# Second attention of a two-layer decoder: the causal mask of the key-major scores as a select on POOL in place of a mask matmul

## The chip, the cores and the metric

One core of a Trainium2 chip. The metric is the device time of one execution in microseconds (us); the kernel before takes 373.02 us, the median of three runs (372.59 to 373.35).

## What is computed

A decoder of two layers on 8 sequences of 128 tokens with 128 features. Each layer is an attention, a cross attention on a context, and a feed-forward part, each followed by a residual add and a normalisation. The change lies in the first attention of the second layer ("the second attention"), 16 heads of 8 features, causal:

```
x = _layernorm(x + _L0_attn_ref(x, ...))      # 16 heads of 64
x = _layernorm(x + _L0_xattn_ref(x, ctx, ctx, ...))
x = _layernorm(x + _L0_ffn_ref(x, ...))       # gated by a softmax of 8
x = _layernorm(x + _L1_attn_ref(x, ...))
x = _layernorm(x + _L1_xattn_ref(x, ctx, ctx, ...))
x = _layernorm(x + _L1_ffn_ref(x, ...))       # quantised to whole numbers

# _L1_attn_ref
scores = jnp.einsum('bhqd,bhkd->bhqk', q, k) / jnp.sqrt(jnp.asarray(D, x.dtype))
causal = jnp.tril(jnp.ones((S, S), dtype=bool))
scores = jnp.where(causal, scores, -jnp.inf)
probs = jax.nn.softmax(scores, axis=-1)
out = jnp.einsum('bhqk,bhkd->bhqd', probs, v)
return out.transpose(0, 2, 1, 3).reshape(B, S, E) @ W_proj + b_proj
```

## The kernel before

Every engine has its program written out by hand, and all of them follow one table of ticks. The first attention takes ticks 0 to 31, one quad (four heads of one pair of sequences) a tick. The second attention begins at tick 32; below its ticks are counted from there as u. It takes the 8 sequences ("batches") one after the other, batch b from u = 4b on, and two ticks later from batch 4 on. A quad is again four heads of a batch, so 32 quads.

The batches come in groups. Groups 0, 1 and 2 hold batches 0 to 2, 3 to 5, and 6 and 7; for each of them a series of "mid" steps does the cross attention and the feed-forward part of layer 0, two normalisations among them, and the keys and queries of the second attention. These leave by DMA to HBM and come back as stacks, Kst and Qst, with high and low parts in rows. Late groups 3 and 4 (batches 0 to 3 and 4 to 7) do the rest of layer 1 in "late" steps. The function `plan` puts each step at a place of the tick table; an engine works through the same table in order and does its share of each step at that place.

A quad of the second attention passes through these steps:

- `scores1` with of_keys false (PE): a mask matmul of 512 columns (L668, ident_b times maskq), then per head one matmul (L676). VectorE takes the row maxima (L1234). After four quads TensorE turns the maxima (L707), and VectorE writes them negated to MR (L1093, L1094).
- `scores1` with of_keys true (PE), from five ticks after the query quad on: the same with keys as rows, so that the exponentials come out ready to be multiplied with the values. A mask matmul with maskk (L668), then per head the scores (L673) and the negated maximum (L674).
- the exponential on ScalarE (L963) into PT, a ring of three slots of 128x512 float32.
- `weigh1` (PE, L690), one tick after the scores of the quad: the exponentials times the values and a column of ones.
- every fourth quad ScalarE copies the sums out (L975), TensorE transposes them (L726), VectorE divides (L1246, L1249), and TensorE, ScalarE and VectorE project and add (L730, L970, L733, L1254).

TensorE's order within a tick is: steps of the table, scores of the query quad, turned maxima, scores of the key quad, steps of the table, `weigh1` and the output of a batch. The three banks 0 to 2 of PSUM go round over the query and key quads.

POOL (GpSimd) sets up constants, among them maskk (L385, L389), and then does only steps of the table: the inverse square root of the normalisations of groups 0 and 3 (`rsqrt`, 16 small instructions, L405 to L413), a sum of bias and rows (`add_bias`, L418), the clearing of the stacks (`zero`, L433), and the rounding of the last weights in three blocks (`ternary`, L425 to L427). For the other groups VectorE does the square root itself (L1155 to L1161). In the second attention's ticks POOL's table reads: `add_bias` of group 2 at u = 7, `zero(2)` at 8, `ternary(0)` at 9, `ternary(1)` at 16, `add_bias` at 21, `ternary(2)` at 22, `rsqrt` of group 3 at 25 and 31. Key quads are scored at u = 5 to 20 (batches 0 to 3) and 23 to 38 (batches 4 to 7).

ScalarE normalises group 3 for the second time at u = 34 (L910), behind its exponential of that tick. The late steps of group 4 begin with L744, which waits for all eight outputs of the second attention.

Of the kernel before, what the change touches and what calls it, by code (L numbers as in the profile page):

```python
# [5 lines left out]
ALU = mybir.AluOpType  # L6
# [8 lines left out]
P = 128  # L15
NB = 8
# [26 lines left out]
T1 = NQ  # L43
# [11 lines left out]
def decoder(nc, x_tok, x_T, ctx_T, wq0, wk0, wv0, wo0, xwq0, xbq0, xwk0, xbk0, xwv0, xbv0,  # L55
# [5 lines left out]
    with ExitStack() as ctx:  # L61
        def sb(name, shape, dt=F32):
            return ctx.enter_context(nc.sbuf_tensor(name, shape, dt))
# [24 lines left out]
        ident = sb("ident", [P, P])  # L88
        ident_b = sb("ident_b", [P, P], BF16)
        maskq = sb("maskq", [P, P], BF16)  # L90
        maskk = sb("maskk", [P, P], BF16)
        res = sb("res", [P, NB, P])
        stats = sb("stats", [P, NB, 6])
        mv = sb("mv", [P, NB, 2])
# [264 lines left out]
        def _(pool):  # L359
# [11 lines left out]
            for m in (ident, ident_b):  # L371
# [10 lines left out]
                               base=-32, pattern=[[-1, H], [0, P]], channel_multiplier=1)\  # L382
                .then_inc(s("setup"), 1)
            pool.memset(maskq[:], 0.0)
            pool.memset(maskk[:], 0.0)  # L385
            link(pool.memset(ones[:], 1.0))
            pool.affine_select(out=maskq[:], in_=maskq[:], compare_op=ALU.is_ge, fill=MASKED,
                               base=0, pattern=[[-1, P]], channel_multiplier=1)
            pool.affine_select(out=maskk[:], in_=maskk[:], compare_op=ALU.is_ge, fill=MASKED,  # L389
                               base=0, pattern=[[1, P]], channel_multiplier=-1)\  # L390
                .then_inc(s("masks"), 1)
            link(pool.memset(af[:, 12288:16384], 0.0))
            for v in VE:
# [73 lines left out]
            def run(t, k):  # L467

                for kind, g, i in TICKS.get((t, k), ()):
                    (mid if kind == "mid" else late)(g, i)  # L470

            for t in range(T1 + TICKS1):
                for k in range(3):
                    run(t, k)


        @block.tensor
        def _(pe):
# [177 lines left out]
            def scores1(w, b, q, of_keys):  # L656

                if w >= 3:
                    pe.wait_ge(s1_free[w % 3], w // 3)
                else:  # L660
                    pe.wait_ge(s("max_done"), NQ)
                g = GROUP[b]
                pe.wait_ge(s(f"stack_in{g}"), 128)
                if of_keys:
                    pe.wait_ge(s("mr1_done"), b + 1)
                t = slice((b - B0[g]) * P, (b - B0[g] + 1) * P)
                K, Q, dst = Kst[g], Qst[g], bank(w % 3)
                mm(dst, ident_b[:], (maskk if of_keys else maskq)[:].unsqueeze(1).broadcast_to([P, 4, P]),  # L668
                   start=True, stop=False)
                for h in range(4):  # L670
                    n, part_ = 4 * q + h, dst[:, h * P:(h + 1) * P]
                    if of_keys:
                        mm(part_, K[:, n, t], Q[:, n, t], start=False, stop=False)  # L673
                        m = mm(part_, En[:, n, :], MR[:, b % 2, :], start=False, stop=(h == 3))  # L674
                    else:
                        m = mm(part_, Q[:, n, t], K[:, n, t], start=False, stop=(h == 3))  # L676
                m.then_inc(s("scores1_done"), 1)

            def weigh1(b, q):

                v, w = 4 * b + q, k_use[b, q]
                pe.wait_ge(s1_free[w % 3], w // 3 + 1)
                if q == 0:
                    pe.wait_ge(s(f"ve_done{GROUP[b]}"), 1)
                    if b:
                        pe.wait_ge(s("o1_out"), b)
                for r in range(4):
                    g = GROUP[b]
                    n = (b - B0[g]) * H + 4 * q + r
                    m = mm(bank(3)[32 * r:32 * r + 32, q * P:(q + 1) * P], VE[g][:, 32 * n:32 * n + 32],  # L690
                           PT[:, v % SLOTS_PT, r * P:(r + 1) * P], start=True, stop=True)
                m.then_inc(s("pv1_done"), 1)
# [760 lines left out]
```

## Time and profile before

| | us |
|---|---|
| median of three runs | 373.02 |
| lowest, highest run | 372.59, 373.35 |
| span of the profiled execution | 371.0 |
| TensorE busy (PE) | 274.2, 74% |
| weight loads (PEld, beside PE) | 222.8, 60% |
| VectorE (DVE) | 250.2, 67% |
| ScalarE (ACT) | 170.9, 46% |
| GpSimd (POOL) | 62.9, 17% |

The profiled execution has a span of 371.0 us, from its first to its last instruction; the profile gives no other time of its own for it, and what lies around the span in the timed runs is 2.0 us (373.02 - 371.0). A busy share is the time in which an engine had an instruction in work. The durations of matmuls are modelled and overlap: the cost of one in a series is the distance from its start to the next start. PEld are weight loads, which run beside the matmuls. "idle before" in square brackets is the time that the engine had nothing to do, with what ended it. The granted clock (PEclk) is 1.00 at 2.4 GHz and 0.50 at 1.2 GHz.

### The profile page before, as it was taken

The numbers are of one execution on the slowest core, as the hardware profiler recorded it, in microseconds if no ns is written. First come the engines' busy times: TensorE is split into PE (matmuls) and PEld (weight loads), VectorE is DVE, ScalarE is ACT, GpSimd is POOL, SyncE is SP. The second block draws the span as 40 slices with busy tenths as digits, with TensorE's granted clock in tenths as the row PEclk, the third lists the DMA queues.
The fourth block names the chain that finished last, engine by engine and source line by source line (L and its number), as shares of the span: only waits on it lengthen the run. The fifth ranks groups of instructions, "written<-read, shape, count | busy, mean of one in ns | idle before, by whom it ended". The sixth has DMA issues, their size and how long they took to land.

```text
span 371.0 us, 6872 instructions
## 1 busy us (share of the span) xinstructions
PE 274.2 (74%) x2578; PEld 222.8 (60%) x2578; DVE 250.2 (67%) x694; ACT 170.9 (46%) x338; POOL 62.9 (17%) x137
## 2 busy tenths in 40 slices
PE   0957678988999989979866697987868874650440
PEld 0946668987899889979755364655545542330120
DVE  4974895589667987586777674657625566767574
ACT  5973663676357944714422343353323352412543
POOL 8700000000003103045150128003300300000300
PEclk9988999999999999989998699898989996975555
DMA  7941023000400050000420043000300000000001
GB/s 264 353 106 31 2 43 72 2 0 16 101 2 0 4 114 2 2 2 29 79 22 2 11 77 42 2 3 7 69 14 0 3 2 0 0 0 1 2 0 57
DMA packets 11568, 14.21 MB, mean 38 GB/s; under 512 B 1552, under 2 KB 9360, under 8 KB 11024
## 3 DMA queue, kind: packets, MB, share of 16 engines
q1 hardware_dynamic: 11536, 13.78, 15.7%
q8 instruction: 21, 0.34, 0.4%
q14 instruction: 11, 0.09, 0.1%
HBM read 8.01 MB, written 1.57 MB: 26 GB/s over the span
## 4 chain that ended last, share of the span: by engine, by line
PE 37%; DVE 34%; DMA 11%; ACT 10%; issue 6%; SPq 2%; ACTq 0%; DVEq 0%
DVE arena L1082 9%; PE PS L562 4%; DMA arena<-arena 4%; PE PS L522 4%; PE PS L588 3%; DMA q_piece<-VN 3%; DVE OT L1124 3%; ACT arena L877 3%; PE PS L485 2%; ACT xt L910 2%; DVE w0l L1071 2%; PE PS L668 2%; DMA arena<-q_piece 2%; DVE stats L1145 2%; PE PS L535 1%
## 5 line engine op out<-in xcount | busy, mean ns | idle before, releaser
L1082 DVE TENSOR_TENSOR arena<-PS,arena 64x512 f16<-64x512 f32 x64 | 44.0, 688 | 4.4 <-ACT arena L877 3.2
L504 PE MATMUL PS<-xh,w0l 128*128 128x256 f32 x96 | 31.5, 328 | 16.7 <-ACT w0h L861 9.3
L877 ACT ACTIVATE arena<-PS 64x512 f16<-64x512 f32 x64 | 37.9, 592 | 12.7 <-PE PS L506 12.0
L963 ACT ACTIVATE PT<-PS 128x512 f32<-128x512 f32 x32 | 19.1, 597 | 45.7 <-PE PS L674 45.7
L405 POOL TENSOR_SCALAR shift<-mv 128x3 f32<-128x3 f32 (+1 forms) x6 | 1.4, 232 | 206.9 <-DVE mv L1148 206.9
L562 PE MATMUL PS<-V,PT 128*128 128x96 f32 x256 | 33.9, 276 | 2.5 <-DVE On L1111 2.5
L562 PEld LDWEIGHTS PS<-V,PT 128*128 128x128 f32 x256 | 31.8, 194 | 3.0 <-ACT PT L897 2.8
L890 ACT ACTIVATE V<-PS 64x256 f32<-64x256 f32 x64 | 24.0, 375 | 19.3 <-PE PS L522 18.6
L504 PEld LDWEIGHTS PS<-xh,w0l 128*128 128x128 f32 x96 | 19.0, 198 | 19.8 <-ACT w0h L861 9.3
L1234 DVE TENSOR_REDUCE rowmax<-PS 128x4 f32<-128x512 f32 x32 | 21.8, 685 | 13.4 <-PE PS L676 13.3
L910 ACT ACTIVATE xt<-res,shift,rstd 128x128 f32<-128x128 f32 x42 | 17.7, 483 | 24.7 <-DVE shift L1161 24.7
L1124 DVE COPY OT<-PS 64x256 f32<-64x256 f32 x64 | 26.9, 420 | 1.4 <-PE PS L580 0.7
L1087 DVE TENSOR_REDUCE rowmax<-PS 128x4 f32<-128x512 f32 x32 | 22.0, 689 | 8.5 <-PE PS L536 8.0
L505 PE MATMUL PS<-xl,w0h 128*128 128x256 f32 x96 | 27.7, 289 | 0.0
L506 PE MATMUL PS<-xh,w0h 128*128 128x256 f32 x96 | 27.7, 288 | 0.0
L897 ACT ACTIVATE PT<-PS 128x512 f32<-128x512 f32 x32 | 19.1, 598 | 12.3 <-PE PS L551 11.3
L549 PE MATMUL PS<-arena 128*128 128x128 f16 x128 | 23.5, 222 | 0.1
L535 PE MATMUL PS<-arena 128*128 128x128 f16 x128 | 19.0, 228 | 6.0 <-DMA arena<-arena 4.8
L550 PE MATMUL PS<-arena 128*128 128x128 f16 x128 | 23.3, 220 | 0.0
L551 PE MATMUL PS<-MR,En 128*128 128x128 f16 x128 | 23.2, 220 | 0.0
L522 PE MATMUL PS<-ident,VN 128*64 128x128 f32 x128 | 21.2, 299 | 2.1 <-ACT VN L880 2.1
L505 PEld LDWEIGHTS PS<-xl,w0h 128*128 128x128 f32 x96 | 19.0, 198 | 0.1
(214 smaller groups left out, 702.6 us busy)
## 6 DMA issues: line engine op xcount, KB each, us to landing
arena<-arena SPq DMA_DIRECT2D x8, 512.0 KB, 4.1
arena<-k_piece SPq DMA_DIRECT2D x8, 96.0 KB
arena<-q_piece SPq DMA_DIRECT2D x8, 96.0 KB
xT<-x_T SPq DMA_DIRECT2D x1, 512.0 KB, 3.7
w<-wk SPq DMA_DIRECT2D x2, 256.0 KB, 4.5
w<-wq SPq DMA_DIRECT2D x2, 256.0 KB, 6.0
w<-wv SPq DMA_DIRECT2D x2, 256.0 KB, 6.3
wo<-wo SPq DMA_DIRECT2D x1, 512.0 KB, 7.0
```

The costliest lines, as they stand in the source:

```text
L504: mm(dst, w0l[:, w, g], xh[:, x], start=True, stop=False)
L505: mm(dst, w0h[:, w, g], xl[:, x], start=False, stop=False)
L506: m = mm(dst, w0h[:, w, g], xh[:, x], start=False, stop=True)
L522: m = turn(bank(at)[0:64, h * P:(h + 1) * P], VN[:, (4 * q + h) * 64:(4 * q + h + 1) * 64], ident[:])
L549: mm(dst, head(KA[p % 2], n), head(QB[p % 2], n), start=True, stop=False)
L550: mm(dst, head(KA[p % 2], n), head(QA[p % 2], n), start=False, stop=False)
L562: m = mm(bank(4)[:, h * VW:(h + 1) * VW], PT[:, Q % SLOTS_PT, h * P:(h + 1) * P], V[:, p % 2, 4 * q + h, :], start=True, stop=True)
L877: m = fn(dst[:, a], src[a * 64:(a + 1) * 64], ACT.Copy)
L890: m = fn(V[a * 64:(a + 1) * 64, p % 2, 4 * q:4 * q + 4, 0:DH0], src[:, :, a, :], ACT.Copy)
L910: fn(xt[:, b, :], res[:, b, :], ACT.Identity, bias=shift[:, b:b + 1], scale=rstd[:, b:b + 1]).then_inc(s(f"xn{g}"), 1)
L1082: m = tt(lower[:, a], src[a * 64:(a + 1) * 64], upper[:, a], ALU.subtract)
L1124: m = V_.tensor_copy(dst[a * 64:(a + 1) * 64, h, 4 * (o % 2):4 * (o % 2) + 4], src[h * 64:(h + 1) * 64, :, a])
```

## The change

The mask matmul of the key quads is gone. The scores of a key quad start each head's 128 columns afresh (start=True), so that ScalarE takes the exponential of unmasked scores. A new POOL instruction per quad then sets to zero every exponential whose key comes behind its query (an affine select on the 128x512 of the PT slot, in place), and `weigh1` waits for the select (semaphore p1_masked) where it waited for the exponential. The select of a tick stands behind the steps at the first place of the table and ahead of those at the second. The constant maskk is no longer made. The query quads keep their mask matmul.

```
-        maskk = sb("maskk", [P, P], BF16)
...
-            pool.memset(maskk[:], 0.0)
             link(pool.memset(ones[:], 1.0))
             pool.affine_select(out=maskq[:], in_=maskq[:], compare_op=ALU.is_ge, fill=MASKED,
-                               base=0, pattern=[[-1, P]], channel_multiplier=1)
-            pool.affine_select(out=maskk[:], in_=maskk[:], compare_op=ALU.is_ge, fill=MASKED,
-                               base=0, pattern=[[1, P]], channel_multiplier=-1)\
+                               base=0, pattern=[[-1, P]], channel_multiplier=1)\
                 .then_inc(s("masks"), 1)
...
+            def keep_causal(u):
+
+                for b in range(NB):
+                    if 5 <= u - u1(b) < 9:
+                        q = u - u1(b) - 5
+                        v, w = 4 * b + q, k_use[b, q]
+                        pool.wait_ge(s1_free[w % 3], w // 3 + 1)
+                        probs = PT[:, v % SLOTS_PT, :].rearrange("p (h q) -> p h q", h=4)
+                        pool.affine_select(out=probs, in_=probs, compare_op=ALU.is_ge, fill=0.0, base=0,
+                                           pattern=[[0, 4], [1, P]], channel_multiplier=-1)\
+                            .then_inc(s("p1_masked"), 1)
+
             for t in range(T1 + TICKS1):
-                for k in range(3):
-                    run(t, k)
+                run(t, 0)
+                if t >= TICKS0:
+                    keep_causal(t - T1)
+                run(t, 1)
+                run(t, 2)
+                if T1 <= t < TICKS0:
+                    keep_causal(t - T1)
...
-                mm(dst, ident_b[:], (maskk if of_keys else maskq)[:].unsqueeze(1).broadcast_to([P, 4, P]),
-                   start=True, stop=False)
+                if not of_keys:
+                    mm(dst, ident_b[:], maskq[:].unsqueeze(1).broadcast_to([P, 4, P]), start=True, stop=False)
...
-                        mm(part_, K[:, n, t], Q[:, n, t], start=False, stop=False)
-                        m = mm(part_, En[:, n, :], MR[:, b % 2, :], start=False, stop=(h == 3))
+                        mm(part_, K[:, n, t], Q[:, n, t], start=True, stop=False)
+                        m = mm(part_, En[:, n, :], MR[:, b % 2, :], start=False, stop=True)
...
-                v, w = 4 * b + q, k_use[b, q]
-                pe.wait_ge(s1_free[w % 3], w // 3 + 1)
+                v = 4 * b + q
+                pe.wait_ge(s("p1_masked"), v + 1)
```

The code behind it moves down by some lines, so the lines of POOL's helpers are four lower and those of the other engines 13 higher.

The order of POOL's instructions from u = 7 to u = 20, before. V MEMSET is `zero(2)`, and wgu_s and wo are the weights of `ternary`:

```order
L418 TENSOR_TENSOR w<-xt,bvx 128x256
L433 MEMSET V 128x4096
L425 TENSOR_SCALAR wgu_s<-wgu_s,wscl 128x512
L426 TENSOR_SCALAR wgu_s<-wgu_s 128x512
L427 TENSOR_SCALAR wo<-wgu_s 128x512
L425 TENSOR_SCALAR wgu_s<-wgu_s,wscl 128x512
L426 TENSOR_SCALAR wgu_s<-wgu_s 128x512
L427 TENSOR_SCALAR wo<-wgu_s 128x512
```

and with the change:

```order
L414 TENSOR_TENSOR w<-xt,bvx 128x256
L476 AFFINE_SELECT PT<-PT 128x512
L429 MEMSET V 128x4096
L476 AFFINE_SELECT PT<-PT 128x512
L421 TENSOR_SCALAR wgu_s<-wgu_s,wscl 128x512
L422 TENSOR_SCALAR wgu_s<-wgu_s 128x512
L423 TENSOR_SCALAR wo<-wgu_s 128x512
L476 AFFINE_SELECT PT<-PT 128x512 x7
L421 TENSOR_SCALAR wgu_s<-wgu_s,wscl 128x512
L422 TENSOR_SCALAR wgu_s<-wgu_s 128x512
L423 TENSOR_SCALAR wo<-wgu_s 128x512
L476 AFFINE_SELECT PT<-PT 128x512 x4
```

The selects are those of quad 3 of batch 0, quad 0 of batch 1, then seven up to quad 3 of batch 2, and the four of batch 3. The memset and the first two blocks of rounding, which followed each other, now stand between them.

The end of POOL's second `rsqrt` of group 3 (u = 31) and the beginning of its third (u = 57), before:

```order
L411 TENSOR_SCALAR nwt<-nwt 128x4
L412 TENSOR_TENSOR rstd<-nwt 128x4
L413 TENSOR_TENSOR shift<-shift,rstd 128x4
L405 TENSOR_SCALAR shift<-mv 128x4
L406 TENSOR_SCALAR nwt<-mv 128x4
```

and with the change:

```order
L407 TENSOR_SCALAR nwt<-nwt 128x4
L408 TENSOR_TENSOR rstd<-nwt 128x4
L409 TENSOR_TENSOR shift<-shift,rstd 128x4
L476 AFFINE_SELECT PT<-PT 128x512 x8
L401 TENSOR_SCALAR shift<-mv 128x4
L402 TENSOR_SCALAR nwt<-mv 128x4
```

The eight selects of batches 6 and 7 now stand behind the second `rsqrt`, the first of them being that of the same tick.

## Rows read from the trace of the kernel before

**Rows 1.** The chain that ended last, in order of time: start us, us, what

```profile
224.37 6.84 DMA arena<-q_piece
...
248.53 0.27 DVE rec L1246
...
267.95 3.67 DMA V<-q_piece
...
296.43 0.97 ACT xt L910 x3
...
313.50 2.08 PE PS L744 x2
```

**Rows 2.** Timeline, PE and ACT, one plain tick: start us, us, engine, instruction, count

```profile
275.92 0.22 PE L674 MATMUL PS<-MR,En 128*128 128x128 f16 x1
...
276.17 0.60 ACT L963 ACTIVATE PT<-PS 128x512 f32<-128x512 f32 x1 [1.79 <-PE PS L674]
...
276.88 0.38 PE L668 MATMUL PS<-maskk,ident_b 128*128 128x512 bf16 x1
...
277.09 0.22 PE L673 MATMUL PS<-arena 128*128 128x128 f16 x1
...
277.63 0.43 PE L690 MATMUL PS<-PT,arena 128*32 128x128 f32 x8
```

**Rows 3.** Busy time by stretch: PE, PEld, DVE, ACT, POOL, then PEclk, DMA share, GB/s

```profile
272.20:275.40 3.20, 3.20 (x26) 1.91 (x25) 0.75 (x2) 0.60 (x1) 0.00 (x0) 0.50 0.02 5
```

**Rows 4.** Timeline, POOL, the selects of the setup

```profile
1.31 0.29 POOL L372 TENSOR_SCALAR_AFFINE_SELECT ident<-ident 128x128 f32<-128x128 f32 x1 [0.25 <-POOL ident_b L370]
...
5.98 2.66 POOL L379 TENSOR_SCALAR_AFFINE_SELECT En<-En 128x2048 f16<-128x2048 f16 x1
...
11.62 0.72 POOL L387 TENSOR_SCALAR_AFFINE_SELECT maskq<-maskq 128x128 bf16<-128x128 bf16 x1
```

**Rows 5.** Timeline, DVE and POOL, where both work at once, and a step of DVE's square root

```profile
6.68 2.49 DVE L1071 TENSOR_TENSOR w0l<-w,w0h 128x512 fp32r<-128x512 f32 x1
...
239.67 0.16 DVE L1159 TENSOR_TENSOR nwt<-nwt 128x2 f32<-128x2 f32 x1
...
265.92 0.69 DVE L1298 TENSOR_TENSOR arena<-w 128x512 f32<-128x512 f32 x1
265.92 0.75 POOL L411 TENSOR_SCALAR nwt<-nwt 128x4 f32<-128x4 f32 x1
```

**Rows 6.** Timeline, POOL, during the second attention

```profile
221.24 3.52 POOL L433 MEMSET V<- 128x4096 f32 x1
224.74 0.70 POOL L425 TENSOR_SCALAR wgu_s<-wgu_s,wscl 128x512 f32<-128x512 f32 x1
...
227.71 0.70 POOL L425 TENSOR_SCALAR wgu_s<-wgu_s,wscl 128x512 f32<-128x512 f32 x1
...
290.38 0.23 POOL L405 TENSOR_SCALAR shift<-mv 128x4 f32<-128x4 f32 x1 [20.91 <-DVE mv L1148]
...
294.60 0.20 POOL L413 TENSOR_TENSOR shift<-shift,rstd 128x4 f32<-128x4 f32 x1
```

**Rows 7.** Timeline, ACT's exponentials and PE, where both meet the work of rows 6

```profile
221.66 0.60 ACT L963 ACTIVATE PT<-PS 128x512 f32<-128x512 f32 x1 [1.16 <-PE PS L674]
...
243.85 0.60 ACT L963 ACTIVATE PT<-PS 128x512 f32<-128x512 f32 x1 [1.20 <-PE PS L674]
...
289.38 0.60 ACT L963 ACTIVATE PT<-PS 128x512 f32<-128x512 f32 x1 [4.56 <-PE PS L674]
...
227.94 0.43 PE L690 MATMUL PS<-PT,arena 128*32 128x128 f32 x8
...
231.34 0.58 PE L668 MATMUL PS<-maskq,ident_b 128*128 128x512 bf16 x1 [1.71 <-DMA arena<-q_piece]
...
247.48 0.42 PE L690 MATMUL PS<-PT,arena 128*32 128x128 f32 x8
...
291.69 0.43 PE L690 MATMUL PS<-PT,arena 128*32 128x128 f32 x8
```

## Prediction

> **What bounds the kernel now.** I read the table of busy shares first, then the chain of waits in order of time, then the timelines of single engines where the second attention runs. The chain shows three stretches in the 90 us that the change touches. Twice TensorE stands still until the stacks of keys and queries of a group have arrived by DMA [rows 1]: for group 1 at 231.21, for group 2 at 271.62. Between and behind these it passes through ticks of TensorE, small VectorE steps (248.53), and at 296.43 ScalarE's second normalisation of late group 3. At 313.50 begins the work that waits for the whole second attention. What the change gives or takes must therefore show before 313.50, and what it takes before 267.95 delays the transfer of group 2 as well, since that transfer starts from the normalised rows of group 2.
>
> In a plain tick TensorE never waits for the exponentials. The last score matmul of a quad starts at 275.92, its exponential runs from 276.17 for 0.60, and the weighing matmul L690 of that quad starts at 277.63, behind the next tick's scores [rows 2]. So there is room of 277.63 - 276.77 = 0.86 us between exponential and use, and the select has to go into it.
>
> **What is taken away.** The mask matmul of the keys issues at 276.88 and the next matmul at 277.09 [rows 2]: 0.21 us of TensorE, 32 times, 6.7 us in all. (The 0.38 of the row is pipelined length.) In stretches where the granted clock is 0.50, as in 272.20 to 275.40 [rows 3], I count twice that, 0.42. Also gone are a 128x128 memset and a 128x128 select in the first 13 us, which nothing waits for until tick 1: nothing. Masks count only where TensorE is on the path. In front of the two DMA waits, and where a normalisation or a row maximum is awaited, they only lengthen a wait. I count as on the path: quad 3 of batch 1 (0.42), quad 0 of batch 2 (0.21), quad 3 of batch 2 (0.21), then quad 3 of batch 4 and quad 0 of batch 5 (0.42 each, at half clock), quad 1 of batch 5 (0.21), and quads 2 and 3 of batch 6 (0.21 each). That is 2.3 us. Quads 0 and 1 of batch 3 would count too (0.4), but they lie behind the wait worked out below, and are lost there.
>
> **What one select costs.** No row has a select of 128x512 float32. The nearest are 0.29 us for 128 elements a partition and 2.66 us for 2048 [rows 4]. A straight line between them gives 0.76 at 512; the 2.66 began while VectorE was busy on two SBUF operands, so I take 0.7. The far end is the 0.72 us of the old mask's own select, the same comparison on only 128 elements [rows 4]: four times that is 2.9 us. I don't take it, because it ran while VectorE's L1071 was going, and the next paragraph shows what that does. The low end is 0.29 + 0.3 = 0.6. A handover costs about 0.08: from 290.38 to 294.60 POOL makes 15 chained steps, 0.28 from start to start, of which 0.20 is the step [rows 6]. From the last score matmul to the weighing: 0.25 + 0.60 + 0.08 + 0.70 + 0.08 = 1.71 us. Before, the weighing came 1.71 after it (277.63 - 275.92), now 1.50 without the mask: in a plain tick 0.2 us of wait eats the 0.21 us won. Most ticks hold another step in the middle and have the room. The select alone is thus about neutral.
>
> The Trainium skill (GPSIMD Engine Reference, "Performance pitfalls for Q7 kernels") gives 2.03 cycles an element for a compare-and-select body that isn't unrolled; as an estimate from it a select would take 0.9 us, and each of the three queue waits below would be 0.2 longer. No run here shows it, and the 2048-element row stands against it.
>
> **What VectorE and POOL do to each other.** L1071 at 6.68 took 2.49 us, where the same shape takes 0.69 in L1298; it ended at 9.17, 0.53 behind the POOL select of 5.98 to 8.64. The other way round, POOL's L411, a step of the same size, took 0.75 at 265.92, exactly while that L1298 (two operands in SBUF) ran [rows 5]. So the two exclude each other for whole instructions. VectorE's reciprocal square root is a row of eleven such small steps, one of them at 239.67 [rows 5], and every later step of its group waits for it. A select that falls into it costs up to 0.7. One falls into the row around 239.67, one or two into the next one, ahead of group 2's transfer. I take 0.5 for the first and 0.4 for the second. The Trainium skill (SBUF — State Buffer, "SBUF: two separate sides") calls the shared port pair an exclusive lock held for the full instruction; by it each of these would be 0.7, and the sum 0.5 us higher. The trace agrees that there is such a lock.
>
> **What is queued on POOL.** This carries the forecast. POOL works in order, and in the order of the change long work stands ahead of selects for which TensorE waits.
>
> First, the memset of 3.5 us and the first 2.97 us block of weight rounding (start to start 224.74 to 227.71) [rows 6]. They ran from 221.24 on. Now the memset comes behind the select of quad 3 of batch 0, whose exponential ends at 222.26 [rows 7], so at 223.0. Then memset 3.5, select 0.8, rounding 3.0, select 0.8: 231.1 is the earliest for the weighing that started at 227.94. TensorE then did 1.69 us of steps, some of it waiting for ScalarE, and stood idle for 1.71 until the DMA's quad at 231.34 [rows 7]. With 1.1 us for those steps, ScalarE being free by then, that quad starts at about 232.2: **+0.9** (it would be +1.5 with the full 1.69).
>
> Second, the second rounding block now comes behind the select of quad 3 of batch 2 (exponential from 243.85) and ahead of that of quad 0 of batch 3. 243.85 + 0.60 + 0.08 + 0.70 + 2.97 + 0.08 + 0.70 + 0.08 = 249.1 against 247.48 [rows 7]: **+1.6**, and the transposes behind it feed VectorE's 248.53 and, over the normalisation, group 2's transfer.
>
> The third rounding block stands ahead of a select too, but in ticks in which no key quad is in flight, and the first square root of group 3 runs inside TensorE's wait for the DMA that ends at 271.62: nothing for either.
>
> Third, the second square root of group 3. It starts when VectorE has its moments (290.38) and ends at 294.80 [rows 6]. The select of quad 0 of batch 6 stands behind it, though its exponential was done at 289.98 [rows 7]. 294.80 + 0.08 + 0.70 + 0.08 = 295.7, against 291.69 for the weighing before [rows 7]: **+4.0**. Behind that weighing TensorE has two more ticks of scores, and ScalarE takes the normalisation at 296.43 only behind the exponential of quad 3 of batch 6; so it moves by all of it. The select lies behind moments that themselves don't wait for it, so nothing circles.
>
> TensorE's clock: behind the 4 us standstill that ends at 271.62 the granted clock was 0.50 for 3.2 us [rows 3]. A new standstill of 4 us should bring the same: two ticks with some 1.5 us of path work become longer. I take **+0.6**, between 0 and 1.5.
>
> **The sum**, in us: +0.9 +1.6 +4.0 (queue), +0.5 +0.4 (VectorE held up), +0.6 (clock), -2.3 (masks) = +5.7. Against the profiled span of 371.0 that is 376.7. The median of the runs is 373.0, 2.0 above the span; so the runs should come to 378.7. Unknowns: the select (0.6 to 0.8) moves it by 0.3 either way, the clock -0.6 to +0.9, the holding up -0.9 to +0.7, and delays that cover each other could take 2.
>
> **Rivals.** (a) *Faster*: POOL's work is early enough, TensorE never waits, the masks are pure gain. Then 2.3 + 0.4 = 2.7 us go: 370.3. For it: POOL is idle most of the stage. Against it: it needs the square root to leave POOL before 290.9, and it can't start before 290.38 [rows 6]. The deciding point is that select; chance 0.07, for an order or a wait that I misread. (b) *The late stall is covered*: if the normalisation at 296.43 were released by something that doesn't pass through the blocked weighing, +4.0 and +0.6 fall away: 1.1 over, 374.1. Chance 0.08. (c) *The comparison itself is slow*: 2.9 us a select, 32 of them are 93 us of POOL, about all the time from shortly before the first row of [rows 7] to 313.50; POOL becomes the bound, ticks of about 2 us become 3, some 20 us more, 395. The rows on the lock explain its 0.72 otherwise: chance 0.03. (d) Gains and waits cancel within 0.2%: 0.04.
>
> **How the numbers follow.** The forecast, both stalls with their sizes, has 0.78. A measurement of this kernel can tell about 0.2%, 0.75 us, from no change. Faster by more is (a), 0.07; within is (d), 0.04; slower is the forecast, (b) and (c), 0.89. The range takes in (b), so it begins at 373.8, and at the other end the bounds of the forecast, 382.5. It leaves out (a), (c) and most of (d), 0.14 together, and the far tails of the forecast.
>
> **What would show it.** Right: selects L476 with a mean near 0.7; TensorE idle ahead of L690 (its new line L703), released by POOL, longest about 4 us near 295; a POOL square root of group 3 directly ahead of it; a smaller one near 247; the normalisation of group 3 at about 302 instead of 296.43; the tail from the end of the second attention as long as before. Wrong: no wait of over 1 us behind POOL, or selects of 1.5 us and more, or the stage before 271 getting shorter.

## The result and the profile after

The change is slower: 382.97 us, the median of four runs (380.34 to 385.22), against 373.19 us for the kernel before, also the median of four. The ratio is 1.0248, 95% interval 1.0188 to 1.0308, so 9.3 us (7.0 to 11.5). Here and in the experiments the medians are over all executions of a kernel, and the ratios leave out the few that took over 1.5% longer than its fastest. The forecast was +5.7 and 378.7: the direction and the mechanism came as forecast, the size was too small. The median lies 0.5 above the range's upper end of 382.5; the ratio, applied to the 373.02 us of the forecast, gives 382.3, just inside.

The four executions were 380.34, 381.22, 384.72 and 385.22 us, with mean granted clocks of 0.879, 0.880, 0.866 and 0.866: the two long ones are those with the lower clock.

The page of the changed kernel's profiled execution (the slowest of the four, 385.22; span 383.4):

```profile
span 383.4 us, 6838 instructions
...
PE 276.4 (72%) x2546; PEld 224.8 (59%) x2546; DVE 253.4 (66%) x694; ACT 171.4 (45%) x338; POOL 82.1 (21%) x167
...
PEclk9986999999999999999978998698889596687555
...
L476 POOL TENSOR_SCALAR_AFFINE_SELECT PT<-PT 128x512 f32<-128x512 f32 x32 | 20.7, 650 | 50.1 <-ACT PT L976 50.1
```

TensorE has 32 mask matmuls fewer and yet 2.2 us more busy time (276.4 against 274.2): part of its work ran at half clock. The PEclk row of the kernel before reads

```profile
PEclk9988999999999999989998699898989996975555
```

A slice is about 9.3 us there and 9.6 in the changed kernel. Before, the row falls to 6 at 204 to 213 us, where normalised rows are awaited, and next at 306 to 315. Now it shows 6 at 240 to 249, 5 at 297 to 307, and 6 twice from 316 to 335. The mean granted clock is 0.866; the median of the runs of before in the experiments is 0.89.

Who waits for the select, first from the view of its own line, then among TensorE's waits from 200 to 345 us (total us, times, longest us):

```profile
L476 POOL TENSOR_SCALAR_AFFINE_SELECT PT<-PT x32: 634/634/852, 216.3 to 314.6; 128x512 f32<-128x512 f32 x32
...
who waited for it (us, times):
  PEld PS L703: 9.2, 6
  PE PS L703: 8.1, 5
```

```profile
PE PS L703 <- POOL PT L476: 8.1, 5, 3.9
```

Of 32 selects, 27 cost TensorE no wait. Five make 8.1 us, but only three of these, 7.0 us together, stand behind other work of POOL: those of quads 0 and 1 of batch 1 and of quad 0 of batch 6. The other two, 0.22 and 0.81 us, are waits for selects that began as soon as their exponential was done (quads 0 and 3 of batch 7). POOL's timeline shows what stands ahead of the three; it answers to [rows 6]:

```profile
223.03 0.63 POOL L476 TENSOR_SCALAR_AFFINE_SELECT PT<-PT 128x512 f32<-128x512 f32 x1 [0.81 <-ACT PT L976]
223.61 3.51 POOL L429 MEMSET V<- 128x4096 f32 x1
227.07 0.63 POOL L476 TENSOR_SCALAR_AFFINE_SELECT PT<-PT 128x512 f32<-128x512 f32 x1
227.69 0.70 POOL L421 TENSOR_SCALAR wgu_s<-wgu_s,wscl 128x512 f32<-128x512 f32 x1
...
229.17 1.50 POOL L423 TENSOR_SCALAR wo<-wgu_s 128x512 bf16<-128x512 f32 x1
230.63 1.22 POOL L476 TENSOR_SCALAR_AFFINE_SELECT PT<-PT 128x512 f32<-128x512 f32 x2
...
294.30 0.23 POOL L401 TENSOR_SCALAR shift<-mv 128x4 f32<-128x4 f32 x1 [4.86 <-DVE mv L1161]
...
298.49 0.20 POOL L409 TENSOR_TENSOR shift<-shift,rstd 128x4 f32<-128x4 f32 x1
298.63 1.23 POOL L476 TENSOR_SCALAR_AFFINE_SELECT PT<-PT 128x512 f32<-128x512 f32 x2
```

And TensorE's timeline, the rows with a wait at the same places and at the steps of the chain behind them ([rows 1, 7] before):

```profile
227.76 0.43 PE L703 MATMUL PS<-PT,arena 128*32 128x128 f32 x8 [1.52 <-POOL PT L476]
231.32 0.43 PE L703 MATMUL PS<-PT,arena 128*32 128x128 f32 x8 [1.66 <-POOL PT L476]
...
243.62 0.45 PE L743 MATMUL PS<-ident,V 128*128 128x128 f32 x1 [2.42 <-DVE V L1262]
...
275.41 0.58 PE L682 MATMUL PS<-maskq,ident_b 128*128 128x512 bf16 x1 [4.06 <-DMA V<-q_piece]
...
299.32 0.65 PE L703 MATMUL PS<-PT,arena 128*32 128x128 f32 x8 [3.86 <-POOL PT L476]
...
309.03 0.43 PE L703 MATMUL PS<-PT,arena 128*32 128x128 f32 x8 [0.22 <-POOL PT L476]
...
315.28 0.42 PE L703 MATMUL PS<-PT,arena 128*32 128x128 f32 x8 [0.81 <-POOL PT L476]
...
324.11 2.07 PE L757 MATMUL PS<-cT,wx 128*128 128x512 f32 x2 [0.45 <-DVE res L1267]
...
334.61 2.04 PE L766 MATMUL PS<-xT,wx 128*128 128x512 f32 x2 [0.78 <-ACT xT L928]
```

The first standstill behind POOL begins 1.5 us before the weighing at 227.76; the second releases at 231.32, where the forecast had worked out 231.1. The largest is at 299.32: the last instruction of the square root begins at 298.49, the select at 298.63, and 0.7 us later TensorE goes on. Of the 12.4 us that this profiled execution is longer than the one before, 3.65 are there when group 2's transfer arrives (275.41 against 271.76), 10.6 when L744, now L757, starts (324.11 against 313.50 in [rows 1]), and the rest comes in the tail. (1.1 us are there before the first select; another profile of the same kernel, below, hasn't got them.) The 0.81 at 315.28 costs nothing further on: from the last exponential to ScalarE's copy of the sums (L975, L988) it takes 3.43 us before and 3.44 now.

Step by step, the same weighing (L690, L703) comes later than before by 0.58 us at 240.78, 3.43 at 249.35, 3.58 at 251.06, 3.70 at 292.98, 7.63 at 299.32 (behind the late wait) and 10.31 at 307.57 (the end of batch 6). So the late wait adds 3.9, and the 8 us behind it add another 2.7, in which no new wait for POOL falls.

Between these places the clock changed. Busy time by stretch (us, then PE, PEld, DVE, ACT, POOL, granted clock, DMA share, GB/s), of the kernel before and then of the changed one:

```profile
243.00:250.00 7.00, 7.00 (x92) 4.97 (x92) 3.76 (x13) 3.13 (x7) 0.00 (x0) 1.00 0.01 4
...
296.40:303.00 6.60, 5.46 (x71) 3.68 (x71) 3.62 (x14) 4.73 (x12) 0.00 (x0) 1.00 0.01 2
```

```profile
243.60:250.60 7.00, 6.45 (x49) 4.54 (x50) 2.18 (x8) 2.56 (x6) 3.92 (x5) 0.53 0.01 2
275.40:281.20 5.80, 5.79 (x51) 3.81 (x52) 1.38 (x2) 1.79 (x3) 1.27 (x2) 0.52 0.00 0
...
294.00:299.30 5.30, 0.62 (x8) 0.45 (x8) 1.38 (x6) 0.77 (x2) 3.79 (x18) 0.88 0.00 0
299.30:309.00 9.70, 8.96 (x77) 5.96 (x77) 3.28 (x8) 4.31 (x10) 2.46 (x4) 0.54 0.01 2
```

Before, the stage from 290 to 303 ran at 1.00. Now TensorE does 0.62 us of work in 5.30 us, and behind that the clock stays near half for 9.7 us of nearly full work. The same 7 us behind L730 (L743) that held 92 matmuls now hold 49 (the counts of the two rows). The kernel before has more stretches at half clock than the 3.2 us of [rows 3], and a longer one among them, behind a wait of 4.68 us that ends at 207.69 (the clock is 0.50 from 207.6 on, 5.9 us in all):

```profile
208.60:213.50 4.90, 4.86 (x14) 2.69 (x15) 2.05 (x5) 1.66 (x3) 0.88 (x1) 0.50 0.06 20
```

The standstill ahead of L743 is behind VectorE, not POOL. In VectorE's square root, about 241 us, there is one step that took 0.60 where its equals take 0.16 ([rows 5]: 239.67), beside the POOL select that runs from 241.55 for 0.63. Its first step took 0.30 for 0.17, beside the select of 239.73 to 240.36:

```profile
240.08 0.30 DVE L1168 TENSOR_SCALAR nwt<-mv 128x2 f32<-128x2 f32 x1
...
241.41 0.16 DVE L1172 TENSOR_TENSOR nwt<-nwt 128x2 f32<-128x2 f32 x1
241.60 0.60 DVE L1173 SCALAR_TENSOR_TENSOR nwt<-nwt 128x2 f32<-128x2 f32 x1
242.23 0.16 DVE L1171 SCALAR_TENSOR_TENSOR nwt<-nwt 128x2 f32<-128x2 f32 x1
```

The reciprocal L1259 and the division L1262 stand behind it on VectorE, and TensorE waits for L1262 until 243.62: its standstill there grew from 1.41 to 2.42 us, and the half-clock stretch is what follows. Of the 1.01 us, 0.57 are the two steps held up (0.44 and 0.13). The other 0.43 are TensorE itself: measured from the start of the square root (239.07 before, 240.08 now) it comes to its wait 0.43 earlier, as much as two mask matmuls of 0.21. So three causes were to be told apart: POOL's queue, VectorE held up by POOL, and the clock.

### The profile page after: what moved, and what is told of

It reads as the page before. It is cut to its first block, busy times and chain, and to the rows that moved or that the text cites. A ratio compares the mean times of both kernels' runs of the same rounds, so it can differ in the third digit from the quotient of the medians.

```text
span 383.4 us, 6838 instructions
## 1 busy us (share of the span) xinstructions
PE 276.4 (72%) x2546; PEld 224.8 (59%) x2546; DVE 253.4 (66%) x694; ACT 171.4 (45%) x338; POOL 82.1 (21%) x167
## 4 chain that ended last, share of the span: by engine, by line
PE 38%; DVE 32%; ACT 11%; DMA 8%; issue 7%; POOL 2%; SPq 1%; ACTq 0%; DVEq 0%
DVE arena L1095 7%; ACT arena L890 4%; PE PS L535 4%; DMA arena<-arena 3%; PE PS L575 3%; PE PS L601 3%; DVE OT L1137 3%; PE PS L498 2%; ACT xt L923 2%; DVE stats L1158 2%; PE PS L517 2%; PE PS L703 2%; DMA w<-wq 1%; DVE arena L1280 1%; PE PS L548 1%
## 5 line engine op out<-in xcount | busy, mean ns | idle before, releaser
L476 POOL TENSOR_SCALAR_AFFINE_SELECT PT<-PT 128x512 f32<-128x512 f32 x32 | 20.7, 650 | 50.1 <-ACT PT L976 50.1
L910 ACT ACTIVATE PT<-PS 128x512 f32<-128x512 f32 x32 | 19.1, 597 | 10.7 <-PE PS L564 9.6
```

## The experiments

The changed kernel once more and eleven variants ran in three sets, the rows of the table in groups of four, each set with its own runs of the kernel before. "Clock" is the median over the runs of the mean granted clock. A difference of two ratios of this table is uncertain by about 0.0045, 1.7 us (2.2 with early_three, whose own interval is wider).

| | median us | before | ratio, 95% interval | clock |
|---|---|---|---|---|
| again | 384.14 | 373.1 | 1.0314 (1.0280 to 1.0349) | 0.866 |
| late_two | 377.81 | 373.1 | 1.0138 (1.0101 to 1.0174) | 0.881 |
| early_three | 381.3 | 373.1 | 1.0260 (1.0210 to 1.0309) | 0.873 |
| both_five | 376.64 | 373.1 | 1.0066 (1.0026 to 1.0106) | 0.887 |
| no_key_mask | 373.62 | 373.66 | 0.9975 (0.9940 to 1.0009) | 0.881 |
| idle_selects | 378.6 | 373.66 | 1.0130 (1.0091 to 1.0168) | 0.891 |
| before_filled | 371.0 | 373.66 | 0.9940 (0.9909 to 0.9971) | 0.903 |
| both_five_filled | 371.0 | 373.66 | 0.9913 (0.9883 to 0.9943) | 0.904 |
| change_filled | 378.36 | 374.13 | 1.0121 (1.0089 to 1.0152) | 0.905 |
| idle_selects_filled | 373.06 | 374.13 | 0.9976 (0.9948 to 1.0004) | 0.908 |
| no_key_mask_filled | 369.35 | 374.13 | 0.9892 (0.9861 to 0.9923) | 0.901 |
| before_filled_more | 367.79 | 374.13 | 0.9821 (0.9784 to 0.9858) | 0.934 |

### The change again: again

No edit.

> The changed kernel as it is, for its spread. Every theory: 9 to 10 us over before (382 to 383); single runs 380 to 385. If the spread comes from TensorE's clock, its runs with a low mean granted clock are the long ones.

384.14 us, 1 us more than expected, 1.0314: the change costs 11.7 us here (10.4 to 13.0), which overlaps the 9.3 of the first measurement (7.0 to 11.5). Four of its six executions have a clock of 0.866 or less, like the two long ones there, and the shortest of the six (382.8) has the highest, 0.875. It is the yardstick of the next three, which ran beside it.

### Back to the mask matmul where POOL is late: late_two, early_three, both_five

The quads in BY_MATMUL keep their mask matmul, wait for the exponential, and have no select. The three kernels differ in that list alone:

```
+BY_MATMUL = ((6, 0), (6, 1))                                   (late_two)
+BY_MATMUL = ((1, 0), (1, 1), (3, 0))                           (early_three)
+BY_MATMUL = ((1, 0), (1, 1), (3, 0), (6, 0), (6, 1))           (both_five)
...
+                        if (b, q) in BY_MATMUL:
+                            continue
                         pool.wait_ge(s1_free[w % 3], w // 3 + 1)
...
-                if not of_keys:
+                by_mm = not of_keys or (b, q) in BY_MATMUL
+                if by_mm:
```

> The changed kernel, but quads 0 and 1 of batch 6, whose selects stand behind POOL's second square root of group 3, keep the mask matmul and have no select. Theory queue: the wait of 3.9 us is gone and with it the half clock behind it, so 5 to 7 us faster than the change, 376 to 378. Rival latency (each select and its lock on VectorE cost a little everywhere, and the queue is hidden): 2 of 32 selects, under 1 us faster, 382.

> The changed kernel, but quads 0 and 1 of batch 1 and quad 0 of batch 3, whose selects stand behind the memset and the two blocks of weight rounding, keep the mask matmul. Theory queue: the stages before the transfer of group 2 come 2 to 2.5 us earlier, 380 to 381. Rival latency: 3 of 32 selects, under 1 us, 382.

> The changed kernel with the mask matmul for all five of these quads and 27 selects. Theory queue: everything that POOL's order costs is gone; what is left is the lock (+0.9 or less) and the masks won (-2): 371.5 to 373.5, no slower than before. Rival latency: 27/32 of 9.8 us stay, 381.

Against again, late_two gives back 6.6 us (1.0314 - 1.0138 of 373), early_three 2.0, give or take 2.2, and both_five 9.3. The 6.6 are as expected. Two quads of 32 hold more than half of the loss. In the stretch where the changed kernel stood still and then ran at half clock, late_two shows:

```profile
290.00:296.00 6.00, 5.32 (x74) 3.81 (x73) 4.04 (x14) 1.75 (x4) 2.38 (x12) 1.00 0.02 4
296.00:306.00 10.00, 7.03 (x103) 4.62 (x95) 5.26 (x17) 6.38 (x14) 4.02 (x9) 1.00 0.01 2
```

A wait of 3.86 us and its +4.0 in the sum can't give back 6.6 by themselves: the clock behind the wait is part of it. The early three gave no more than their two waits of 1.5 and 1.7 us. Behind them TensorE waits for a DMA anyway; early_three's wait for group 2's transfer is 5.09 us, where again's is 4.35.

With everything gone that POOL's queue made TensorE wait for, both_five is still 0.66% slower than before, 2.5 us, although 27 mask matmuls are missing; the queue theory had asked for 371.5 to 373.5. Its profiled execution is a long one (379.54 us against the median of 376.64), so it shows what can happen and doesn't stand for the 2.5 us. It has the VectorE step and the low clock, first VectorE and POOL, then the stretch:

```profile
240.64 0.16 DVE L1185 TENSOR_TENSOR nwt<-nwt 128x2 f32<-128x2 f32 x1
240.84 0.60 DVE L1186 SCALAR_TENSOR_TENSOR nwt<-nwt 128x2 f32<-128x2 f32 x1
```

```profile
240.79 0.63 POOL L483 TENSOR_SCALAR_AFFINE_SELECT PT<-PT 128x512 f32<-128x512 f32 x1 [1.19 <-ACT PT L989]
```

```profile
243.00:250.00 7.00, 6.48 (x47) 4.34 (x47) 2.01 (x8) 2.26 (x6) 3.42 (x4) 0.51 0.01 2
```

### Each half of the change alone: no_key_mask, idle_selects

The first is the kernel before without the key quads' mask matmul; it leaves out the causal mask of the key-major scores. The second is the kernel before, complete, with one select per key quad on a part of a tile that nobody uses then (On), for which nobody waits:

```
no_key_mask:
-                mm(dst, ident_b[:], (maskk if of_keys else maskq)[:].unsqueeze(1).broadcast_to([P, 4, P]),
-                   start=True, stop=False)
+                if not of_keys:
+                    mm(dst, ident_b[:], maskq[:].unsqueeze(1).broadcast_to([P, 4, P]), start=True, stop=False)
idle_selects:
+                        pool.wait_ge(s1_free[w % 3], w // 3 + 1)
+                        one = On[:, 0:8, :].rearrange("p n d -> p (n d)").rearrange("p (h q) -> p h q", h=4)
+                        link(pool.affine_select(out=one, in_=one, compare_op=ALU.is_ge, fill=0.0, base=0,
+                                                pattern=[[0, 4], [1, P]], channel_multiplier=-1))
```

> The kernel before without the mask matmul of the key quads and without any select; the causal mask of the key-major scores is left out of the computation. What the 32 masks are worth by themselves. The prediction's count: 2.7 us faster than before, 370.3. Rival clock: with less work TensorE's standstills begin earlier and grow, the granted clock falls to half behind the one near 241 (1.4 us before) too, and the gain is given back: within 1 us of before, 372 to 374.

> The kernel before with its mask matmuls, plus a select of 128x512 on a dead tile at each of the 32 places of the change, after the same exponential; nobody waits for them. Only what POOL's selects do to VectorE (and to POOL's own later work) is left. Theory lock: VectorE's small steps are held up by 0.4 to 0.6 us for each select that falls into them, 1 to 2 us over before in all, 374 to 375, more if the longer standstill lets the clock fall. Rival: no effect of the lock on the path, 373.

The masks alone are worth 0.9 us, and the interval (2.2 faster to 0.3 slower) holds no gain at all too; the prediction's 2.7 lie outside it. TensorE arrives earlier at its waits and stands longer in them. In its timeline the two waits for the transfers, 1.71 and 4.22 us in the kernel before, are

```profile
231.30 0.38 PE L669 MATMUL PS<-maskq,ident_b 128*128 128x512 bf16 x1 [3.13 <-DMA arena<-q_piece]
...
272.61 0.58 PE L669 MATMUL PS<-maskq,ident_b 128*128 128x512 bf16 x1 [4.97 <-DMA V<-q_piece]
```

and the mean clock is lower, 0.881. The wait for VectorE near 241 grew from 1.41 to 1.84 us with no select on POOL at all, and behind it the granted clock from 242 to 246 us is 0.57 in place of 1.00.

The idle selects cost 4.9 us (3.4 to 6.3), more than the 1 to 2 expected of the lock, though no engine waits for one. Here is VectorE in it, a square root of group 2, and POOL beside it:

```profile
217.91 0.64 DVE L1168 TENSOR_SCALAR nwt<-mv 128x2 f32<-128x2 f32 x1
...
220.55 0.48 DVE L1174 SCALAR_TENSOR_TENSOR shift<-mv,rstd 128x2 f32<-128x2 f32 x1
```

```profile
217.90 0.64 POOL L479 TENSOR_SCALAR_AFFINE_SELECT On<-On 128x512 f32<-128x512 f32 x1 [0.52 <-ACT PT L976]
220.39 0.63 POOL L479 TENSOR_SCALAR_AFFINE_SELECT On<-On 128x512 f32<-128x512 f32 x1 [1.86 <-ACT PT L976]
```

Two steps that take 0.17 and 0.16 took 0.64 and 0.48. TensorE's standstills behind VectorE grow from 0.91 to 1.71 us (221.69) and from 1.41 to 2.28 (241.38). Two hold-ups of some 0.8 us don't make 4.9 by themselves; the clock could.

### Is it the clock? Fillers in the standstills: before_filled, both_five_filled

A filler is a 128x128 matmul of constants, in front of a wait of TensorE, into a piece of PSUM that is written anew afterwards. It adds work and computes nothing. `rows1` and `rows2` are waits for normalised rows, `stack1` and `stack2` those for the transfers, `out1` and `out7` those for the divided sums:

```
+FILL = {'rows1': 60, 'stack1': 22, 'rows2': 24, 'stack2': 60, 'out7': 28}      (before_filled)
+            def fill(place, dst):
+                for i in range(FILL.get(place, 0)):
+                    mm(dst, ident_b[:], maskq[:], start=True, stop=True)
...
+                if (b, q, of_keys) == (B0[g], 0, False):
+                    fill(f"stack{g}", bank(w % 3)[:, 0:P])
                 pe.wait_ge(s(f"stack_in{g}"), 128)
```

both_five_filled has these and `out1`, 28, on top of both_five.

`rows1` isn't where the expectation puts it. In before_filled its 60 matmuls run from 192.45 and fill the wait that was 3.12 us in front of 196.58. The one of 4.68 us "near 204" stays (4.69), and from 205.8 to 211.5 the clock is 0.56.

> The kernel before with small matmuls (128x128, bf16, into a part of a bank that is rewritten) in five standstills of TensorE: 60 before the rows of group 1 near 204, 22 and 60 before the stacks of groups 1 and 2, 24 before the rows of group 2 near 253, 28 before the last output near 309. Theory clock: the granted clock stays at full behind them and the stretches that ran at half clock (207.6 to 213.5, 231.7 to 234.6, 254 to 258, 272.2 to 275.4, 313.5 to 317.5) shrink: 4 to 7 us faster than before, 366 to 369. Rival: the clock falls all the same or the stretches hide behind other engines: 373 or a little slower.

> The kernel of run both_five (27 selects, five quads with the mask matmul) with the same fillers and 28 more in the standstill near 242, ahead of the transposed output of batch 1. Theory clock: what both_five lost against before (3.5 us) was half clock behind that standstill; with the clock held up it comes to the filled kernel before plus 0 to 1.5 us. Rival latency: it stays 3 us and more behind the filled kernel before.

194 useless matmuls make the kernel before 2.2 us faster (0.9940; 1.1 to 3.4). That is less than the 4 to 7 expected; the stretch that wasn't reached is one reason. The wait for group 2's transfer now leaves 1.03 us idle, and L753 (here L765) starts at 275.01 where it started at 281.03:

```profile
267.28 0.39 PE L679 MATMUL PS<-maskq,ident_b 128*128 128x512 bf16 x1 [1.03 <-DMA V<-q_piece]
...
275.01 1.10 PE L765 MATMUL PS<-xT,wx 128*128 128x512 f32 x2 [0.16 <-ACT xT L927]
```

both_five_filled comes to the same 371.0, and its 2.5 us over the kernel before are gone: with fillers in both, 27 selects in place of 27 matmuls give -0.0027, 1.0 us, which can't be told from nothing.

### The terms of the sum with fillers on both sides: change_filled, idle_selects_filled, no_key_mask_filled

```
+FILL = {'rows1': 60, 'w10': 20, 'w11': 22, 'out1': 28, 'w30': 20, 'rows2': 24, 'stack2': 60, 'w60': 60, 'out7': 28}
...
+                    fill(f"w{b}{q}", bank(3)[:, q * P:(q + 1) * P])
                 pe.wait_ge(s("p1_masked"), v + 1)
```

That is change_filled; `w60` is in front of the wait for the select of quad 0 of batch 6. It has no `stack1`, since the changed kernel doesn't wait there, so it fills four of before_filled's five places and five of its own. Every filler ahead of a select still leaves some idle time behind it (0.41 to 0.54 us), so these fillers delay nothing. idle_selects_filled has before_filled's places and `out1`, no_key_mask_filled the same with `stack1` 40 (and leaves out the mask as above).

> The changed kernel with filler matmuls (their output is not used) where its TensorE stands still: in the five standstills that before_filled fills and ahead of the select-fed quads of batches 1, 3 and 6. Clock theory: queue stalls and lock stay, the clock's share of the change's 11 us is given back: 3 to 5 us faster than again (384.1), so 379 to 381, granted clock 0.89 or more. Rival, that stalls alone make the 11 us: 383 to 385.

> idle_selects (nobody waits for its 32 selects) with filler matmuls in the standstills. It was 4.9 us over the kernel before. If most of that is the clock falling after standstills that VectorE's hold-up lengthened, it is now only 1 to 2.5 us over before_filled (371.0), so 372 to 373.5. If the hold-up on VectorE alone makes it, 4 to 5 us over: 375 to 376.

> no_key_mask (the causal mask of the key-major scores is left out, no select either) with filler matmuls in the standstills. If the clock and longer standstills ate the 2.3 us that the eight mask matmuls take, they now come back: 2 to 2.7 us faster than before_filled (371.0), so 368.3 to 369. If the mask matmuls were beside other work all along: 371.

Against before_filled: change_filled +0.0181, idle_selects_filled +0.0036, no_key_mask_filled -0.0048. In us: +6.8, +1.3 and -1.8, each give or take 1.7. By their own medians change_filled (378.4) and no_key_mask_filled (369.35) lie just beside what was expected, idle_selects_filled within it. The change itself fell from +11.7 to +4.5 over the kernel before. Its wait for the late select is still there (a fill of 3.51 us, then 0.54 idle), and behind it the clock is full:

```profile
290.46 3.51 PE L497 MATMUL PS<-maskq,ident_b 128*128 128x128 bf16 x60
294.51 0.42 PE L715 MATMUL PS<-PT,arena 128*32 128x128 f32 x8 [0.54 <-POOL PT L477]
```

```profile
294.50:304.00 9.50, 7.23 (x101) 5.08 (x101) 5.15 (x16) 5.05 (x11) 3.18 (x5) 1.00 0.01 2
```

101 matmuls in 9.5 us, where the changed kernel did 77 in 9.7. The wait for quad 0 of batch 3, of which the changed kernel showed nothing, is there: a fill of 1.28 us, then 0.52 idle ahead of L715 at 245.79.

Two of the three effects moved beyond their uncertainty, as the clock theory asked: the change lost 5.0 us of its 11.7 (give or take 2.1), and the idle selects 3.5 of their 4.9 (give or take 2.1). So most of the 4.9 was clock; what is left, 1.3 give or take 1.7, goes to VectorE held up and is not clear of nothing. The third isn't shown: the masks are worth 0.9 without fillers and 1.8 with them, and these two can't be told apart. One reserve: before_filled and these three ran in different sets, and are compared by their ratios to the kernel before.

### A faster kernel: before_filled_more

before_filled and fillers at four late places (ahead of the transposes of the hidden rows of two batches, ahead of L753 and of the query rows of late group 4):

```
-FILL = {'rows1': 60, 'stack1': 22, 'rows2': 24, 'stack2': 60, 'out7': 28}
+FILL = {'rows1': 60, 'stack1': 22, 'rows2': 24, 'stack2': 60, 'out7': 28, 'down1': 24, 'x4': 10, 'q4': 30, 'down3': 130}
```

> before_filled with filler matmuls also in the late standstills of the last layers. If late standstills still cost clock: 1 to 3 us faster than before_filled (371.0), so 368 to 370. If the fillers only stand in the way there: 371 or more.

367.79 us, 0.9821: 6.7 us faster than the kernel before, and 4.4 than before_filled, more than the 1 to 3 expected. It computes all of the reference, with the mask matmul. The late L753 (L766), at half clock before_filled's 2.04, is back to 1.10, and six late us are at full clock:

```profile
320.31 1.10 PE L766 MATMUL PS<-xT,wx 128*128 128x512 f32 x2 [0.22 <-ACT xT L930]
```

```profile
320.00:326.00 6.00, 5.25 (x46) 3.52 (x44) 2.85 (x7) 0.88 (x2) 0.00 (x0) 1.00 0.00 0
```

The same stretch of before_filled:

```profile
320.00:326.00 6.00, 3.80 (x11) 2.06 (x11) 2.02 (x4) 0.00 (x0) 0.00 (x0) 0.50 0.00 0
```

## Why the prediction was right and wrong

- **TensorE's clock (+0.6, between 0 and 1.5): the term that was too small.** I took the 3.2 us at 0.50 behind the existing 4 us standstill [rows 3] as the price of one new one. It was the shortest stretch to take: the same kernel ran at half clock for 5.9 us from 207.6 on. In the changed kernel the stretches behind new or longer waits are 7.0, 5.8 and 9.7 us, and there are more in the tail (L753 of late group 4 takes 2.04 for 1.10). Two measures of it agree. By the profile, half clock adds 1.9 us behind L743 (from 1.58 to 3.43) and 2.7 behind the late wait; this profile is of the longest execution. By the ratios, fillers take 7.2 us off the changed kernel (1.0314 - 1.0121) and 2.2 off the kernel before, so the clock's part of the change is 5.0, give or take 2.1. With the first measurement in place of again it is 2.5, give or take 2.8.
- **The queue on POOL (+0.9, +1.6, +4.0): right for the largest, in place and size.** The extra wait behind the square root is 3.86 for 4.0, and a select takes 0.63 for 0.7. The first term was too large: the release came at 231.32 (forecast 231.1), but the quad of the DMA started at 232.70, 1.4 later than before, of which 1.1 were there before the first select. The second, behind the second rounding block, cost nothing in the changed kernel: the weighing at 251.06 is 3.58 later than before, the one ahead of it had been 3.43 later already, at half clock. In change_filled, at full clock, it is a wait of 1.8 us. Giving back the five quads gives back 9.3 of 11.7 us, with the clock behind the waits.
- **What VectorE and POOL do to each other (+0.5, +0.4): right in kind.** The step held up was forecast at 239.67 and came at 241.60, with a smaller one at 240.08, 0.57 us together for 0.5. What was not forecast is what a half microsecond there does: with 0.43 from the missing masks it lengthened a standstill of TensorE to 2.4 us, and 7 us at half clock came behind. Idle selects cost 4.9 in all, with fillers 1.3 (give or take 1.7). The sentence of the Trainium skill (SBUF — State Buffer, "SBUF: two separate sides") that the port pair is locked for the full instruction would have given 0.5 more. The 0.60 and 0.64 beside selects of 0.63 agree with a lock that lasts as long as the instruction.
- **Up to group 2's transfer the sum was right by luck.** The terms ahead of it are +0.9 +1.6 +0.5 +0.4 and 0.84 for three entries of the masks, +2.6. Measured are 3.65, less the 1.1 from before the first select: also 2.6. But two of the parts, +0.9 and +1.6, hardly came, and half clock behind L743 came in their place.
- **The masks (-2.3): not shown as a gain.** I counted them at their places on TensorE's path. Without fillers they are worth 0.9 (interval through zero), with fillers 1.8, give or take 1.7; 1.7 is what the same count gives at full clock (2.3 less 0.21 for each of the three at half clock). "Masks count only where TensorE is on the path" leaves out what they do to the clock off the path: near 241 the missing masks alone made the standstill 1.84 us, with a clock of 0.57 behind it. That this ate their gain is likely, and not measured apart.
- **The sum.** The other terms, with the masks at full clock, were forecast as 6.5 + 0.9 - 1.7 = 5.7, and with fillers on both sides the change costs 6.8, give or take 1.7. What is missing from the forecast is the clock. 5.7 and 5.0 make 10.7, but that checks nothing further, as the 5.0 is got from the 11.7.
- **What would show it.** Of the signs of "right", the select of 0.63, the wait of 3.86 behind POOL near 299 and the square root directly ahead of it came; the smaller wait near 247 didn't. The normalisation of group 3, forecast for about 302, came at 306.00, and "the tail as long as before" was wrong by 1.8 us in this profile. None of the signs of "wrong" came. A select in a plain tick, "about neutral", was: 27 of 32 made no wait.
- **The rivals.** (a), faster with POOL never late, falls by the waits of L703. (b), the late stall covered, falls by late_two, which gives back 6.6. (c), 2.9 us a select, falls by the 0.63, and (d), no difference, by the ratio.

What stays open: how the 5.0 us of clock divide among the standstills. No kernel filled one of them alone. Nor is it shown why executions of one kernel differ in clock, 0.861 to 0.880 for the changed one; with the clock its time goes from 380.3 to 385.2 us, and so may the 9.3 and the 11.7 of the two measurements.

## What to carry to other kernels

Before work moves to an engine that is idle on average, read its queue at the instants where the result is needed: three of 32 selects made 7.0 of the 8.1 us of waiting here, behind work that nobody was in a hurry for. Then price every new or longer standstill of TensorE with the stretch at half clock behind it, and not with the wait alone. Read all such stretches of a profile, since one alone can be the shortest. Time saved ahead of a wait lengthens the standstill, and need not show in the total. To find out what the clock costs, fill the standstills of both kernels with matmuls of constants and compare again; here that also gave the fastest kernel.

## What the runs showed of the hardware

- A half-clock stretch wasn't of one length, and not set by the wait ahead of it alone: 3.2 and 5.9 us in the kernel before, behind 4.22 and 4.68 us of idle time, and in the changed one 5.8, some 7 and 9.7, behind idle times of TensorE of 4.06, 2.42 and 3.86 us in this order. The Trainium skill (TensorE: Matmul & The Clock Gate, "HAM oscillation — how this bites in real kernels") tells of a matmul kernel whose waits for DMA brought the half clock back in every tile, and counts what the half clock costs apart from the waits. These rows agree, and here waits for other engines did the same as waits for DMA.
- A standstill of 1.41 us ahead of L730 left the clock at 1.00 in the kernel before; at the same place one of 1.84 in no_key_mask was followed by 0.57, and one of 2.41 in both_five by 0.51. The same wait could go either way: 1.86 us near 220 left the clock at 1.00 in one profile of the changed kernel (221.5 to 224.5 us), and was followed by 0.50 in another, again (the same stretch).
- VectorE's steps on 128x2 elements, among them one with a single SBUF operand (L1168), waited out a whole POOL select: 0.64 and 0.60 us for 0.16 to 0.17.
- A select on 128x512 float32 takes 0.634 us at the least and 0.852 at the most; on 128 elements a partition it took 0.29 [rows 4].
- 388 matmuls without a use, in nine waits of TensorE, made a kernel 1.8% faster (before_filled_more), with a mean clock of 0.934 for 0.89.
